# Attention stage of a ViT tower: context sums turned by VectorE and DMA, a new table of steps, guard rows on GpSimd's queue, reordered sync queue

## The reference, cut to what matters

```python
emb = jnp.einsum('bsf,fd->bsd', x, W) + pe[None]       # token embedding, H
# the kernel feeds attention with layernorm(emb): n0
Q = x @ Wq.T + bq;  K = x @ Wk.T + bk;  V = x @ Wv.T + bv
Q = Q.reshape(B * H, L, dh)      # 8 heads of 16; the plain reshape cuts the
K = K.reshape(B * H, L, dh)      # tokens into 8 groups of 128, so a "head" is
V = V.reshape(B * H, L, dh)      # a group of 128 tokens x 8 slices of features
attn = jax.nn.softmax(jnp.einsum('bqd,bkd->bqk', Q, K) * dh ** -0.5, axis=-1)
context = jnp.einsum('bqk,bkd->bqd', attn, V).reshape(B, L, D)
out = context @ Wo.T + bo + x
out = (out - mu) / jnp.sqrt(var + LN_EPS) * gamma + beta
# next: scores = x @ attn_w + attn_b  (its normalised input is made in this stage)
```

## Time and profile before

| | us |
|---|---|
| median of 3 runs | 1568.18 |
| the profiled execution, its own time | 1566.77 |
| its span (first to last instruction) | 1564.5 |
| PE busy (9689 matmuls) | 1250.5 |
| ACT busy | 1012.1 |
| DVE busy | 989.6 |
| POOL busy | 520.9 |
| exponentials of the first stage (L343, 512 times) | 491.2 |

### The profile page before, as it was taken

How to read it: one execution, slowest core, us unless ns; L and a number is a source line. 1 busy time by engine, 2 the same in 40 slices (tenths; PEclk the granted TensorE clock), 3 DMA queues, 4 the chain that set the end, 5 groups by cost and what they waited for, 6 DMA issues and landing times. The chain is left out here.

```text
span 1564.5 us, 30966 instructions
## 1 busy us (share of the span) xinstructions
PE 1250.5 (80%) x9689; PEld 826.3 (53%) x9689; DVE 989.6 (63%) x2772; ACT 1012.1 (65%) x1358; POOL 520.9 (33%) x456
## 2 busy tenths in 40 slices
PE   3599999999999999926999994888870699999930
PEld 2244444444444444414777773777760577777720
DVE  5256666666666664333777876788641589999932
ACT  0387778777778888902888883444410688888820
POOL 3212222222222221210000001278775066666654
PEclk9599999999999999967999996888855799999975
DMA  3542424242425252001111100011112455555519
GB/s 89 88 97 46 93 49 97 45 93 49 95 47 97 42 102 36 2 9 48 34 48 34 47 7 12 4 40 46 46 47 101 113 146 147 151 149 151 151 44 299
DMA packets 134465, 118.97 MB, mean 76 GB/s; under 512 B 30459, under 2 KB 112310, under 8 KB 134350
## 3 DMA queue, kind: packets, MB, share of 16 engines
q1 hardware_dynamic: 114798, 93.72, 26.5%
q0 software_dynamic: 9216, 16.94, 3.2%
q10 hardware_dynamic: 10336, 6.82, 2.2%
HBM read 76.61 MB, written 42.37 MB: 76 GB/s over the span
## 5 line engine op out<-in xcount | busy, mean ns | idle before, releaser
L343 ACT ACTIVATE a_probs<-a_psS 128x1024 f32<-128x1024 f32 x512 | 491.2, 1031 | 125.5 <-PE a_psS L426 98.4
L438 PE MATMUL a_psO<-a_probs,a_v 128*32 128x256 f32 x4096 | 282.5, 395 | 24.7 <-DVE a_o_sb L643 23.9
L807 ACT ACTIVATE f_g_hi<-f_psH,f_b_hid 128x512 fp32r<-128x512 f32 x288 | 200.6, 696 | 56.4 <-PE f_psH L71 49.6
L922 DVE TENSOR_TENSOR f_g_lo<-f_g,f_g_hi 128x512 fp32r<-128x512 f32 x288 | 197.7, 688 | 54.6 <-ACT f_g L809 52.5
L1744 POOL DMA_INDIRECT result<-f_out,f_idx x160 | 184.2, 1151 | 118.4 <-DVEq L1768 62.8
L426 PE MATMUL a_psS<-a_qs,a_ks 50*128 50x512 f32 x1024 | 193.8, 457 | 26.6 <-issue 12.4
L809 ACT ACTIVATE f_g<-f_psH,f_b_hid 128x512 f32<-128x512 f32 x288 | 199.8, 694 | 0.0
L438 PEld LDWEIGHTS a_psO<-a_probs,a_v 128*32 128x32 f32 x4096 | 108.7, 111 | 170.1 <-issue 89.2
L426 PEld LDWEIGHTS a_psS<-a_qs,a_ks 50*128 50x128 f32 x1024 | 79.2, 191 | 99.6 <-ACT a_probs L343 46.4
L69 PE MATMUL f_psH<-f_x_hi,f_w_lo 128*128 128x512 f32 x288 | 125.3, 435 | 2.9 <-DVE f_w_lo L64 2.6
L69 PE MATMUL f_psY<-f_g_hi,f_w_lo 128*128 128x512 f32 x288 | 117.1, 407 | 8.5 <-DVE f_w_lo L64 6.2
(11 more groups left out here) (296 smaller groups left out, 2152.7 us busy)
## 6 DMA issues: line engine op xcount, KB each, us to landing
f_raw<-W SPq DMA_DIRECT2D x80, 256.0 KB
a_qs<-qparts SPq DMA_DIRECT2D x96, 128.0 KB, 4.7
a_ks<-kparts SPq DMA_DIRECT2D x84, 128.0 KB, 4.7
f_rows<-queue SPq DMA_DIRECT2D x40, 260.0 KB, 2.7
qparts<-a_parts SPq DMA_DIRECT2D x16, 512.0 KB, 2.8
f_raw<-w SPq DMA_DIRECT2D x32, 256.0 KB, 2.6
kparts<-a_parts SPq DMA_DIRECT2D x14, 512.0 KB, 3.2
out_y<-result SPq DMA_DIRECT2D x8, 512.0 KB, 14.0
```

The costliest lines, as they stand in the source:

```text
L343: nc.scalar.activation(probs[u % NPR][:, :], psS[score_buffer(u)][:, :, :].rearrange("p a n -> p (a n)"), ACT.Exp).then_inc(exp_done, 1)
L438: last = nc.tensor.matmul(psO[32 * g:32 * g + 32, a * HALF:(a + 1) * HALF], v[par][:, 2 * hp + p, kt, :], probs[u % NPR][:, cols:cols + HA ...
L807: nc.scalar.activation(g_hi[i][:, n, :], psH[n][:, :], ACT.Gelu, bias=b_hid[i][:, n:n + 1])
L922: nc.vector.tensor_tensor(g_lo[i][:, n, :], g[:, n, :], g_hi[i][:, n, :].bitcast(F32), ALU.subtract).then_inc(lo_done, 1)
```

## The change

**Sums.** `turn`, `turn_back` and `evacuate` are gone. DVE now moves `psO` out with its own 32x32 block transpose (`o_t`), divides there, transposes the blocks back (`o_n`), and SP stores the 4 strips to DRAM (`store_sums`, 32 KB each) and loads them as one 128x256 tile `ctxT` (`load_sums`, 128 KB). PE only projects, two pairs late (`LATE = 2`), at the first burst of a pair, between the scores and the weigh.

**Steps.** The tables have new bursts: the steps of `STEPS` stand at 1, 3, 5, ... 19 and at 27 and 29, the flag at 22 instead of 26; the finishing of the halves is spread over other bursts, and the second half of the lower half's finishing moves into the next batch.

**DMA.** The guard rows are sent by GpSimd's queue. SP stores q and k of a half, then loads them; the loads are 4 instead of 6 for the same bytes (32 partitions hold high and low interleaved), counted by one semaphore per half, so that unit 0 waits for the first half only. Between them SP carries the trips of the sums. GpSimd clears fewer columns of V (those behind the 16 values of a head become ones).

```diff
@@ tables
-    PIECES = ((0, 0, 0), (0, 1, 16), (1, 0, 32))
+    HIGH = (0, 1)
-    STEPS = {0: ("E", 0), 4: ("E", 1), 6: ("T", 0), 8: ("q", 0), 12: ("k", 0), 14: ("T", 1), 16: ("q", 1), 20: ("k", 1),
-             22: ("N", 0), 24: ("N", 1), 28: ("v", 0), 30: ("v", 1)}
+    STEPS = {1: ("E", 0), 3: ("E", 1), 5: ("T", 0), 7: ("q", 0), 9: ("k", 0), 11: ("T", 1), 13: ("q", 1), 15: ("k", 1),
+             17: ("N", 0), 19: ("N", 1), 27: ("v", 0), 29: ("v", 1)}
-    TURN, BACK, PROJECT = 1, 2, 3
-    RESCUE = 26
+    LATE = 2
+    RESCUE = 22
-    UPPER = {3: "add_bias", 7: "normal", 10: "moments", 11: "second", 13: "score"}
-    LOWER = {21: "add_bias", 23: "normal", 26: "moments", 27: "second", 29: "score"}
-    APPLY = {1: 0, 5: 1}
+    UPPER = {2: ("moments", 0), 4: ("second", 0), 6: ("score", 0), 10: ("add_bias", 1), 12: ("normal", 1), 18: ("moments", 1), 23: ("second", 1),
+             25: ("score", 1)}
+    LOWER = {26: ("add_bias", 0), 28: ("normal", 0)}
+    APPLY = {2: 0, 8: 1}
@@ loads of q and k
+        def load_parts(eng, b, par, kind, ch):
+            out, dram = ((qparts_out, dq), (kparts_out, dk))[kind]
             eng.wait_ge(out, (b * CPB + ch) * 16 + 32)
-            src = dram[ch].rearrange("(j d) a p t -> d j a p t", d=DH)
+            both = dram[ch].rearrange("(j d) a p t -> p (d a) j t", d=DH)
+            high = dram[ch].rearrange("(j d) a p t -> p d a j t", d=DH)[:, :, HIGH[kind], :, :]
             for p in range(2):
-                for piece in PIECES:
-                    rows = slice(64 * p + piece[2], 64 * p + piece[2] + DH)
-                    eng.dma_start((qs, ks)[kind][par][rows, :, ch * HALF:(ch + 1) * HALF].bitcast(F32),
-                                  src[:, :, piece[kind], p, :]).then_inc(stack_in, 16)
+                for row, src in ((0, both[p]), (2 * DH, high[p])):
+                    rows = slice(64 * p + row, 64 * p + row + src.shape[0])
+                    eng.dma_start((qs, ks)[kind][par][rows, :, ch * HALF:(ch + 1) * HALF].bitcast(F32), src).then_inc(stack_in[par][ch], 16)
@@ sync queue
+            def store_sums(pair):
+                sp.wait_ge(norm_done, pair + 1)
                 for p in range(2):
+                    for cc in range(2):
+                        row = 64 * p + 32 * cc
+                        sp.dma_start(dctx[pair % 2][64 * cc:64 * cc + 64, p, :].rearrange("(i d) t -> d i t", d=DH),
+                                     o_n[row:row + DH, :].rearrange("d (i t) -> d i t", t=P)).then_inc(ctx_out, 16)
+            def load_sums(pair):
+                sp.wait_ge(ctx_out, (pair + 1) * 4 * 16)
+                if pair:
+                    sp.wait_ge(op_done, pair)
+                sp.dma_start(ctxT[:, :, :], dctx[pair % 2]).then_inc(ctx_in, 16)
@@ gpsimd
+                    if more and m == RESCUE - 1:
+                        send_guard(pool, b + 1, 1 - par)
-                nc.gpsimd.memset(v[par][:, :, :, :], 0.0)
-                pool.drain()
-                nc.gpsimd.memset(v[par][:, :, :, DH:DH + 1], 1.0)
+                nc.gpsimd.memset(v[par][:, :, :, DH:], 1.0)
@@ tensor
                 if u == 0:
-                    pe.wait_ge(stack_in, (b + 1) * STACK)
-                    pe.wait_ge(guard_in, (b + 1) * GUARD)
+                    wait_guard(pe, b)
+                    q, r = divmod(m, BPP)
+                    pair = b * HP + (q - LATE)
+                    if r == 0 and pair >= 0:
+                        pe.wait_ge(psA_free, uses.next())
+                        project(pair)
                     for u in (2 * m, 2 * m + 1):
                         weigh(b, par, u)
@@ vector
-                nc.vector.tensor_copy(o_sb[:, :], psO[:, :]).then_inc(o_evac, 1)
+                nc.vector.transpose(o_t[:, :, :].rearrange("p k e -> p (k e)"), psO[:, :]).then_inc(o_evac, 1)
             def divide(pair):
+                dve.drain()
+                nc.vector.reciprocal(rden[:, :].unsqueeze(2), o_t[:, :, DH:DH + 1])
+                dve.drain()
+                nc.vector.tensor_tensor(o_t[:, :, 0:DH], o_t[:, :, 0:DH], rden[:, :].unsqueeze(2).broadcast_to([P, CH // 32, DH]), ALU.mult)
+                dve.drain()
+                if pair:
+                    dve.wait_ge(ctx_out, pair * 4 * 16)
+                nc.vector.transpose(o_n[:, :], o_t[:, :, :].rearrange("p k e -> p (k e)")).then_inc(norm_done, 1)
```

173 lines of the change are left out of this document (94 added, 79 removed).

## The result

| | before | after |
|---|---|---|
| median, us | 1567.7 (1566.65 to 1569.17, 4 runs) | 1541.67 (1538.5 to 1542.75, 4 runs) |
| the profiled execution, its span | 1566.77, 1564.5 | 1541.9, 1540.1 |
| first scores | 60.91 | 55.65 |
| from there to the last burst of batch 6 | 545.4 | 524.3 |
| last batch, to the end of its last weigh | 63.2 | 61.3 |

The ratio is 0.983 [0.9813, 0.9847]: 26 us faster, where I had forecast 45. The time lies in the range; the gain is little over half of it.

What follows compares the result with a forecast made beforehand. PE was taken to set the pace. From 1566.77 us, seven batches at -4.5 (-32), clock -8, start -8.6 and last batch with tail +3.5 gave -45.1, so 1521 us; range 1502 to 1544.

Steps and rivals of the forecast that it cites:

- (a): Bursts with turn and turn_back: both leave PE, -3.84 us a batch.
- (b): Bursts without an extra: in five of them ACT's floor takes some back, +1.1 us a batch.
- (c): PE's wait for the copy out of `psO` vanishes, with a 0.71 us transpose instead: -3.4 us a batch.
- (e): The flag's load: the flag is made three bursts ahead instead of two, -0.7 us a batch.
- the slower rival: DVE's transposes out of `psO` cost four times as much, 2.8 us each: 1606 us, chance 7%.
- (d): PE's wait for the divided sums vanishes, their 10 us DRAM trip hidden by eight bursts: -0.5 us a batch.
- Four loads for six bring nothing: Loads of q and k: fewer loads for the same bytes cost and bring nothing.
- (f): New waits of PE for DVE at steps q and burst 8's projection: +2.8 us a batch, bounds 0 and 5.6.
- (g): Clock in the batches: PE's longest pauses get shorter, -8 us in all, bounds 0 and -10.8.
- (h): Ahead of the first scores: GpSimd sends the guard rows at once, -8.6 us, bounds 0 and -9.2.
- (i): Last batch -2.7 us, and the tail behind its last weigh +6.2 us; together +3.5.
- the second rival: DVE sets the pace of bursts 1 to 16 and the clock gives only half: 1545 us, chance 20%.

Runs made afterwards that it cites:

- experiment 1: The changed kernel with the sums' store and load issued on SP's queue ahead of the second half's loads of q and k: 1518.08 us, ratio 0.9689.
- experiment 5: The changed kernel with the old six loads per kind and half instead of four: 1576.13 us, ratio 1.005.
- experiment 9: The kernel of experiment 1 with six loads per kind and half instead of four: 1523.57 us, ratio 0.9732.
- Experiment 3: The changed kernel with score, bias and normal of the upper half two bursts later: 1534.71 us, ratio 0.9798.
- Experiment 8: The kernel of experiment 1 with only the upper half's score moved from burst 6 to 8: 1524.96 us, ratio 0.9732.
- experiment 11: The kernel of experiment 1 with the upper half's score, bias, normal and moments at later bursts, and a DVE drain before the last batch's add_input: 1505.14 us.
- Experiment 6: The changed kernel with the prologue's loads of the second half issued only when the guard rows have landed: 1540.34 us, ratio 0.9833.

## Why the prediction was right, and where its steps failed

- **(a), (b), (c), (e)** held. Bursts with a projection and no wait take 2.30, none takes 2.04 or 2.24; plain runs take 1.76 to 1.84; the transposes take 0.71 us each and `weigh` waits for none of them; the flag's burst takes 2.87 to 3.04, with a pause of some 1.2 where (e) left 1.07. The slope of two narrow rows gave the cost of a wide one to 1%. So the slower rival (2.8 us) is out, and the Trainium skill's figure (VectorE: DVE Perf Modes, The three transpose paths) paid four times is too: the tile is one operation whose cost follows the columns (1.06 ns each from 64 to 256 on 32 partitions, 1.07 from there to 512 on 128).
- **(d) is the step that failed.** I compared the trip of the sums, 10 us, with eight bursts or 17 us. I named "SP's waits for q and k ahead of it" and gave them no number, and I took DVE's part as if nothing stood ahead of the divide and the landings as those of DMAs alone. Measured (469.99 to 489.87 above), DVE took 6.2 us instead of 2, SP's queue 2.2 ahead of the first store, and the issues and landings beside the loads 11.5 instead of 8. Together that was 10 us more, against a slack of 7. It cost 23.8 us at burst 24; experiment 1 gives 22 back by order alone. In my list this stood as 1% within the slower rival, and at four times a batch; it came once a batch, always where the two loads of the second half fall.
- **"Four loads for six bring nothing"** failed with it. I looked at the bytes, and neither at the issues that stand ahead of others on the same queue (1.2 us a batch) nor at how much later a store lands beside six loads (2.3 us a batch): 34 us in experiment 5, and 7, hardly clear of noise, in experiment 9 where nobody waits behind them.
- **(f)**: the waits were 16.8 us in seven batches, 2.4 each against the 2.8 forecast, 1.3 at burst 8. Right in size; but in five batches the lower clock came right behind the wait at burst 8, and in a sixth at burst 13, which I had not put there: burst 8 took 14.6 us over 2.30 in all, 7.9 of it waiting. Experiments 3, 8 and 11 show the cause: DVE is short between bursts 5 and 15 and has room behind them.
- **(g)**: -8 did not come as a clock of 0.98; the windows stand at 0.93 to 0.97, since d and f made new pauses. With both gone (experiment 11) it is 1.00.
- **(h)**: -5.3 instead of -8.6, and not for the reason given. I charged the wait to SP's queue; the rows left 2.7 us earlier and were then held by the second half's loads, the bound that I had named for zero gain. Experiment 6 shows the 5.5 us that were still there for the first scores, of which ACT's late table lets 3.2 through. (The terms of (h) add up to 52.0 and not 52.3, and the four issues took 2.30 us and not 3.9.)
- **(i)** held: -1.9 and +5.7 against -2.7 and +6.2 (10.6 less 0.4 is 10.2 and not 10.4, so the sum itself gives +6.0).

Together: the seven batches were to gain 40 us (32 and 8) and gained 21.1. Burst 24 cost 23.8 us more than forecast and burst 8 some 7 (14.6 against 7.2), 31 in all, so the other bursts were some 12 better than my sum. PE's busy time fell by 23.1 us (503.74 to 480.68), where (a) and (g) have 35: the lower clock behind the waits of bursts 24 and 8, 8.1 and 6.7 us, can account for the 12 that are missing. Its idle time rose by 1.9 where the other terms have -5; since 15.7 of it are the wait for `ctxT`, the rest of it was 9 better than forecast, 3 of that in (f). The start cost 3.3 more. No run has the new way of the sums or the new tables alone, so what each is worth is read from burst lengths and not from a time.

The time is in the range, but not for a reason that I had given. The forecast was 1521, and the upper bound of 1544 stands there for the second rival (1545), whose mechanism, DVE setting the pace of bursts 1 to 16, made 7 us, the late trip of the sums 24. That these summed to less than the range is luck. My own signs say so: a batch was to take at most 75 us and takes 74.7 to 75.7, and the projection was to wait for `ctxT` at the end alone.

## What to carry to other kernels

A trip through DRAM on a queue that others use has no length of its own: write down what is issued ahead of it, with the time of each issue and of each wait, and put the small DMAs that someone waits for ahead of the large ones nobody waits for yet. The number of DMAs counts, not only their bytes: by their issues on the queue, and by how much later what travels beside them lands. Before moving a piece of an engine's work to cure a late step, find the stretch in which the engine has room; inside a full stretch the wait only moves, and behind a pause of PE the lower clock can add half of it again or nearly all (here 8.1 us behind 15.7 of waiting at burst 24, 6.7 behind 7.9 at burst 8).
